# Two chained per-pixel channel mixes: four rows interleaved in SBUF, another way to layer 1's column matrices, fills at once, row products spread out

## The chip, the cores and the metric

The kernel runs on one core of a Trainium2 chip. A core has five engines that run on their own and wait for one another through semaphores: TensorE (PE; its weight loads are shown as PEld), VectorE (DVE), ScalarE (ACT), GpSimd (POOL) and SyncE (SP, which here issues all DMAs). The time is device microseconds of one execution. Kernel before: 859.1 us, median of 3 runs (857.77 to 862.08).

## The reference, cut to what matters

Two layers of the same form, each with its own factors, on x of 16 channels by 1024 rows (T) by 1024 columns (S), all float32:

```python
def layer(x, w, qw1, qw2, kw1, kw2, qdd, kdd):      # x: 1, 16, T, S ; M = N = 16, I = 2
    ret = einsum('BGMTS,GMN->BGNTS', x, w + eye)
    ret += einsum('BGITS,BTGIM->BGMTS', einsum('BGMTS,BTGIM->BGITS', x, qw1), qw2)   # per row t
    ret += einsum('BGITS,BSGIM->BGMTS', einsum('BGMTS,BSGIM->BGITS', x, kw1), kw2)   # per column s
    return ret + x * qdd[t] + x * kdd[s]
out = layer(layer(x, L0...), L1...)
```

So for each pixel (t, s) the 16 channels are multiplied by a 16x16 matrix that is a row matrix R[t] plus a column matrix C[s]. R[t] = qw1 qw2 (rank 2) plus the diagonal qdd; C[s] = kw1 kw2 (rank 2) plus w, the identity and the diagonal kdd.

## The kernel before, in words

**Tiling.** The rows are cut in 8 blocks of 128, a block in 16 chunks of 8 rows. The 1024 columns are cut in 8 eighths of 128 (`COLS`). A partition holds one channel of one eighth: 8 x 16 = 128 partitions. In the free dimension a chunk lies as [row group][column][row within the group], and `PAIR` rows make a group, here 2. One chunk is 4 KB a partition. `X` holds the block (and layer 0's result), `Y` the partial sums, `OUT` four slots for results.

**Four kinds of matmul.** A matmul's weights are small channel matrices placed on the diagonal of a larger one (`spread_quarter`, `spread_whole`: a compact row or column matrix times a mask).

- `t1(k, j)`: R of layer 0 on chunk j of block k. For each of 8 rows four matmuls of 64x64 weights on 64 columns, at the four quarters of the array. The moving columns of one row lie `PAIR` floats apart. Each matmul is two instructions, so 64 a chunk. ACT copies the result to `Y` (`t1_copies`).
- `s1(k, g)`: C of layer 0 on 4 of 64 column places, 16 matmuls of 64x64 weights on the block's 128 rows; the rows of one column lie in runs of `PAIR` floats. DVE adds the result to `Y` (`add_columns`).
- `s2(k, g)`: C of layer 1 on `Y`, the same shape; ACT copies it back to `X` (`s2_copies`).
- `t2(k, g)`: R of layer 1 on `Y`, whole 128x128 weights, 4 rows; DVE adds the result to what s2 left in `X` and writes `OUT` (`add_rows`).

A block's s phase is s1 and s2 in turn, 16 groups each, s2 two groups behind. Its t phase is, for each of 16 chunks, two t2 groups and the t1 chunk of the next block. The last t phase has no t1. PSUM banks are used in rings of two (PA for t1 and s2, PB for s1 and t2, where t2 takes four).

**Who makes the weights.** GpSimd makes WA (for t1, s2) and the odd WB, DVE the even WB, each four slots ahead.

**The queue of SP.** In the t phase, for each chunk: wait for DVE's row adds, store the chunk, load chunk o + 3 of the next block. After chunk 9 (`PROD_STORE`) it also waits for the next block's row products, stores both layers' products to DRAM and loads the next factors `QP`. At the s phase SP loads the first three chunks of the following block and reads the products back, replicated over the eighths, into `RT`. The products themselves (`products_of`: for each layer two multiplies, a sum, a diagonal add) stand in DVE's queue after chunk 6 (`PROD_STEP`).

**Start-up.** ACT writes w, the identity and kdd of all columns into `RS` (`base`). TensorE copies the factor kw2 from 8 partitions to 128 by a matmul with a selection matrix (`fill`, 512 values a time, 16 fills for two layers), DVE multiplies each by kw1 and adds it to RS (`column_unit`). Four fills come first, then one after each t1 chunk, since four banks of PB take them in turn.

Of the kernel before, what the change touches and what calls it, by code (L numbers as in the profile page):

```python
# [50 lines left out]
def cross_conv_kernel(nc, x, first_rows, row_params, col_left, col_right, w, products, out):  # L51
# [13 lines left out]
    with ctx:  # L65
# [374 lines left out]
        def _(dve):  # L440
# [31 lines left out]
            def row_matrices(l, before):  # L472
                shape = [P, CH, CH]
                q1, q2 = ([QP[:, l, (RANK * j + i) * CH:(RANK * j + i + 1) * CH] for i in range(RANK)]
                          for j in range(2))
                prod = PROD[:, l]
                for i in range(RANK):
                    nc.vector.tensor_tensor(prod[:, i], q1[i].unsqueeze(2).broadcast_to(shape),  # L478
                                            q2[i].unsqueeze(1).broadcast_to(shape), ALU.mult).then_inc(prod_step, 1)
                dve.wait_ge(prod_step, before + RANK)  # L480
                nc.vector.tensor_tensor(prod[:, 0], prod[:, 0], prod[:, 1], ALU.add).then_inc(prod_step, 1)  # L481
                dve.wait_ge(prod_step, before + RANK + 1)
                diagonal = prod[:, 0].rearrange("t c n -> t (c n)")[:, 0:CH * CH:CH + 1]
                nc.vector.tensor_tensor(diagonal, diagonal, QP[:, l, 2 * RANK * CH:PARAMS], ALU.add
                                        ).then_inc(prod_ready, 1)

            def products_of(number):
                dve.wait_ge(q_loaded, DMA * (number + 1))
                if not first(number):
                    dve.wait_ge(prod_stored, DMA * LAYERS * number)  # L490
                for l in range(LAYERS):
                    row_matrices(l, (RANK + 1) * (LAYERS * number + l))

# [240 lines left out]
```

## Time and profile before

| | before |
|---|---|
| median of 3 runs | 859.1 us |
| the profiled execution, and its span | 858.88 us, 857.1 us |
| PE busy / PEld busy | 766.5 / 704.4 us |
| DVE / POOL / ACT busy | 546.1 / 513.6 / 393.6 us |
| HBM read / written | 85.25 / 69.34 MB, 180 GB/s over the span |
| mean granted TensorE clock | 0.976 |

The span is the time from the first to the last instruction of the profiled execution; 1.8 us lie around it. Busy time of TensorE holds modelled ends of pipelined matmuls, so that the distance from one group's start to the next one's start is the better measure of its pace. The granted clock is 1.00 at 2.4 GHz and 0.50 at 1.2 GHz. A bracket at the end of a timeline row is the idle time ahead of it, and what ended it.

### The profile page before, as it was taken

What the parts mean: (1) busy time and instruction counts of PE and PEld (TensorE: products, weight loads), DVE (VectorE), ACT (ScalarE), POOL (GpSimd) and SP (SyncE); (2) the same over time, 40 slices, a digit from 0 to 9 for tenths busy, and PEclk for the clock granted to TensorE, in tenths of its full rate; (3) what the DMA queues carried; (4) which work ended last, traced back from release to release, by engine and by line L of the source; (5) the groups of instructions that cost most, each with busy time, mean ns of one, the idle gap of its engine ahead of it and who ended that gap; (6) DMA issues with size and microseconds to landing.
All of it is one profiled execution on the core that took longest, in us unless ns stands there. A gap on an engine that the chain in (4) does not pass through costs nothing.

```text
span 857.1 us, 42054 instructions
## 1 busy us (share of the span) xinstructions
PE 766.5 (89%) x18464; PEld 704.4 (82%) x18464; DVE 546.1 (64%) x809; ACT 393.6 (46%) x673; POOL 513.6 (60%) x456
## 2 busy tenths in 40 slices
PE   5998899799898999797998899979998889988998
PEld 2658799699787988797987898868998779877997
DVE  3338557468474866665676675837758566665668
ACT  6224563247432583225833466325743267324640
POOL 2326577467665677555766567646776567765733
PEclk9999999999999999989999999999999999999999
DMA  9804318952568618774098723785167840985026
GB/s 190 296 3 100 93 59 309 295 185 66 200 213 296 180 25 293 232 282 101 3 333 237 265 75 131 277 277 183 44 245 257 297 110 6 341 251 184 4 116 278
DMA packets 76045, 157.09 MB, mean 183 GB/s; under 512 B 39768, under 2 KB 40792, under 8 KB 73944
## 3 DMA queue, kind: packets, MB, share of 16 engines
q1 hardware_dynamic: 75888, 154.61, 55.5%
q8 instruction: 146, 2.39, 1.1%
q14 instruction: 11, 0.09, 0.0%
HBM read 85.25 MB, written 69.34 MB: 180 GB/s over the span
## 4 chain that ended last, share of the span: by engine, by line
POOL 34%; PE 25%; issue 24%; DVE 7%; DMA 5%; SPq 2%; POOLq 1%; ACT 1%; DVEq 0%; ACTq 0%
POOL WA L200 19%; POOL WB L208 9%; PE PB L655 7%; PE PA L607 7%; POOL WB L200 6%; PE PA L642 5%; PE PB L624 4%; DMA X<-in_x_dram 3%; DVE OUT L524 3%; PE PB L592 3%; DVE WB L208 2%; SPq L240 1%; DVE PROD L478 1%; DMA RT<-products 1%; DVE PROD L481 1%
## 5 line engine op out<-in xcount | busy, mean ns | idle before, releaser
L524 DVE TENSOR_TENSOR OUT<-PB,X 128x512 f32<-128x512 f32 x256 | 172.4, 686 | 185.0 <-PE PB L655 141.0
L402 ACT ACTIVATE Y<-PA 128x512 f32<-128x512 f32 (+1 forms) x256 | 147.3, 634 | 306.7 <-PE PA L607 306.7
L412 ACT ACTIVATE X<-PA 64x512 f32 (+3 forms) x384 | 232.7, 606 | 118.5 <-PE PA L642 111.8
L655 PE MATMUL PB<-Y,WB 128*128 128x128 f32 x2048 | 272.6, 286 | 1.7 <-issue 1.0
L655 PEld LDWEIGHTS PB<-Y,WB 128*128 128x128 f32 x2048 | 248.8, 193 | 15.8 <-issue 6.2
L208 POOL TENSOR_TENSOR WB<-RT,mask 128x512 f32<-128x512 f32 x128 | 156.3, 1221 | 106.1 <-PE PB L655 102.6
L511 DVE TENSOR_TENSOR Y<-PB,Y 128x512 f32 (+1 forms) x256 | 164.8, 685 | 80.7 <-PE PB L624 69.5
L607 PEld LDWEIGHTS PA<-X,WA 64*64 64x64 f32 x8192 | 149.4, 145 | 78.1 <-issue 37.8
L642 PE MATMUL PA<-Y,WA 64*64 64x128 f32 x4096 | 190.9, 311 | 20.7 <-issue 14.3
L607 PE MATMUL PA<-X,WA 64*64 64x64 f32 x8192 | 170.1, 234 | 44.0 <-DMA X<-in_x_dram 25.3
L200 POOL TENSOR_TENSOR WA<-RS,mask 128x512 f32<-128x512 f32 x128 | 139.4, 1089 | 110.7 <-PE PA L642 85.4
L624 PE MATMUL PB<-X,WB 64*64 64x128 f32 x4096 | 189.1, 311 | 14.6 <-DVE Y L511 9.3
L200 POOL TENSOR_TENSOR WA<-RT,mask 128x512 f32<-128x512 f32 x128 | 140.6, 1102 | 85.4 <-PE PA L607 47.1
L642 PEld LDWEIGHTS PA<-Y,WA 64*64 64x64 f32 x4096 | 163.7, 139 | 25.7 <-issue 16.4
L624 PEld LDWEIGHTS PB<-X,WB 64*64 64x64 f32 x4096 | 162.2, 139 | 18.7 <-issue 18.4
L208 DVE TENSOR_TENSOR WB<-RT,mask 128x512 f32<-128x512 f32 x128 | 102.8, 803 | 0.0
L200 POOL TENSOR_TENSOR WB<-RS,mask 128x512 f32<-128x512 f32 x64 | 80.7, 1262 | 33.6 <-PE PB L655 16.7
L200 DVE TENSOR_TENSOR WB<-RS,mask 128x512 f32<-128x512 f32 x64 | 69.2, 1082 | 0.0
L501 DVE TENSOR_TENSOR PB<-PB,RT 128x512 f32<-128x512 f32 x16 | 11.2, 700 | 31.1 <-PE PB L592 31.0
L478 DVE TENSOR_TENSOR PROD<-QP 128x256 f32<-128x256 f32 x32 | 22.3, 735 | 0.0
L592 PE MATMUL PB<-OUT,RT 8*128 8x512 f32 x16 | 15.4, 1104 | 5.4 <-DMA OUT<-in_right_dram 5.4
L419 ACT ACTIVATE RS<-RT,delta 128x128 f32<-128x128 f32 x32 | 12.5, 574 | 4.6 <-DVE RT L559 4.6
(24 smaller groups left out, 62.4 us busy)
## 6 DMA issues: line engine op xcount, KB each, us to landing
X<-in_x_dram SPq DMA_DIRECT2D x128, 512.0 KB, 6.0
out_dram<-OUT SPq DMA_DIRECT2D x128, 512.0 KB, 4.5
RT<-products SPq DMA_DIRECT2D x15, 1024.0 KB
products<-PROD SPq DMA_DIRECT2D x16, 128.0 KB, 8.2
RT<-products SPq DMA_DIRECT2D x1, 768.0 KB
QP<-in_rows_dram SPq DMA_DIRECT2D x8, 80.0 KB, 3.5
RT<-in_left_dram SPq DMA_DIRECT2D x1, 384.0 KB
RT<-products SPq DMA_DIRECT2D x1, 256.0 KB
```

Source lines behind the costliest of these rows:

```text
L200: engine.tensor_tensor(dst.rearrange("q (t a n) -> q t a n", t=CHUNK, a=PARTS), r, m, ALU.mult).then_inc(ready, 1)
L208: engine.tensor_tensor(dst.rearrange("q (t p n) -> q t p n", t=FEW, p=EIGHTHS), r, m, ALU.mult).then_inc(ready, 1)
L402: nc.scalar.activation(rows_of(Y, k, j)[:, :, WIDE * h:WIDE * (h + 1), :].rearrange("q a s c -> q a c s"), PA[HALVES * (j % RING) + h][:, ...
L412: nc.scalar.activation(columns_of(block_of(X, k), dst, WIDE * i + NARROW * g), by_columns(PA[HALVES * (g % RING) + i][src, :]), ACT.Copy). ...
L478: nc.vector.tensor_tensor(prod[:, i], q1[i].unsqueeze(2).broadcast_to(shape), q2[i].unsqueeze(1).broadcast_to(shape), ALU.mult).then_inc(p ...
L511: nc.vector.tensor_tensor(at, by_columns(PB[HALVES * (g % RING) + h][:, :]), at, ALU.add).then_inc(b_done, 1)
L524: nc.vector.tensor_tensor(rows(OUT[:, o % OUT_SLOTS]), PB[g % SLOTS][:, :].rearrange("q (a c s) -> q a c s", a=FEW2, c=PAIR), rows(rows_of ...
L592: nc.tensor.matmul(PB[u % FILLS][:, :], sel[0:EIGHTHS], KR[l][place // per][:, BANK * (place % per):BANK * (place % per + 1)], start=True, ...
L607: last = nc.tensor.matmul(PA[HALVES * (j % RING) + h][part(o), WIDE * r:WIDE * (r + 1)], matrix(WA[:, j % SLOTS], h, r), rows_of(X, k, j)[ ...
L624: last = nc.tensor.matmul(PB[HALVES * (g % RING) + h][part(o), ROWS * v:ROWS * (v + 1)] .rearrange("q (a c) -> q a c", c=PAIR), matrix(WB[ ...
L642: last = nc.tensor.matmul(PA[HALVES * (g % RING) + i][part(h ^ i), ROWS * v:ROWS * (v + 1)] .rearrange("q (a c) -> q a c", c=PAIR), matrix ...
L655: last = nc.tensor.matmul(PB[g % SLOTS][:, COLS * r:COLS * (r + 1)], WB[:, g % SLOTS, P * r:P * (r + 1)], rows_of(Y, k, t2_chunk(o))[:, (i ...
```

## The change: what it does

`PAIR` becomes 4: four rows are interleaved in X, Y and OUT, and in the host's layout of x and of the output. Counts of instructions in the two phases stay.

Layer 1's column matrices no longer go through TensorE. Its kw2 is loaded already replicated over the 16 channels (`load_right`, two DMAs of 1 MB) into the spare ends of Y and X, and DVE multiplies and adds there in operations of 1024 elements (`columns_of_layer1`). Layer 0's eight fills go into all eight banks at once, before the first t1.

The row products of the next block are one operation per chunk, from chunk 2 to chunk 9 (`product_op`), and are stored after chunk 11.

```diff
-PAIR = 2
+PAIR = 4
-UNITS = LAYERS * QUARTERS * RANK
-FILLS = 4
+UNITS = QUARTERS * RANK
+SIDE = COLS // 2
-PROD_STEP = 6
-PROD_STORE = 9
+PROD_FIRST = 2
+PROD_OPS = 4
+PROD_STORE = 11
...
+            def load_right(h):
+                sp.dma_start(KR1[h].rearrange("q i s n -> q (i s n)"),
+                             col_right1[h].unsqueeze(1).broadcast_to([EIGHTHS, CH, RANK * SIDE * CH])
+                             ).then_inc(right_loaded[1 + h], DMA)
...
-            for h in range(2):
-                load_right(1, h, right_loaded[1 + h])
-            load_q(0)
             load_x(0, 1)
             sp.wait_ge(first_stored, DMA)
             load_rows(BLOCKS * LAYERS, 0, 0, FIRST_ROWS, rt_first)
             load_x(0, 2)
             load_rows(BLOCKS * LAYERS, 0, FIRST_ROWS, ROWS - FIRST_ROWS, rt_loaded[0])
-            for j in range(3, CHUNKS):
+            load_x(0, 3)
+            for h in range(len(KR1)):
+                load_right(h)
+            load_q(0)
+            for j in range(4, CHUNKS):
                 load_x(0, j)
...
+            def columns_of_layer1(h):
+                shape = [P, SIDE, CH]
+                part = slice(SIDE * h, SIDE * (h + 1))
+                dve.wait_ge(right_loaded[1 + h], DMA)
                 for i in range(RANK):
+                    chained(nc.vector.tensor_tensor(KR1[h][:, i], KL[:, 1, i, part].unsqueeze(2).broadcast_to(shape),
+                                                    KR1[h][:, i], ALU.mult))
+                chained(nc.vector.tensor_tensor(KR1[h][:, 0], KR1[h][:, 0], KR1[h][:, 1], ALU.add))
+                dve.wait_ge(base_ready, LAYERS * CH)
+                nc.vector.tensor_tensor(RS[:, 1, part, :], KR1[h][:, 0], RS[:, 1, part, :], ALU.add
+                                        ).then_inc(rs1_done, 1)
...
-                    if more and o == PROD_STEP:
-                        products_of(k + 1)
+                    n = o - PROD_FIRST
+                    if more and 0 <= n < LAYERS * PROD_OPS:
+                        product_op(k + 1, n // PROD_OPS, n % PROD_OPS)
...
+            for u in range(RING * HALVES):
+                unit_product(u)
             for u in range(UNITS):
-                column_unit(u)
+                unit_sum(u)
+                if RING * HALVES + u < UNITS:
+                    unit_product(RING * HALVES + u)
+            dve.wait_ge(right_done, UNITS)
             for g in range(0, SLOTS, 2):
                 s1_weights(nc.vector, g, wb_even)
-            products_of(0)
+            for n in range(LAYERS * PROD_OPS):
+                product_op(0, n // PROD_OPS, n % PROD_OPS)
+            for h in range(len(KR1)):
+                columns_of_layer1(h)
...
             pe.wait_ge(sel_ready, 1)
-            for u in range(FILLS):
+            pe.wait_ge(right_loaded[0], DMA)
+            for u in range(UNITS):
                 fill(u)
             for j in range(CHUNKS):
                 t1(0, j)
-                if FILLS + j < UNITS:
-                    fill(FILLS + j)
```

TensorE at the start, before. L592 is a fill (its bank PB, its source in OUT), L607 a matmul of t1.

```order
L592 MATMUL PB<-OUT,RT 128x512 [waits right_loaded0,sel_ready]
L592 MATMUL PB<-OUT,RT 128x512 [waits right_loaded0] x3
L607 MATMUL PA<-X,WA 64x64 [waits wa_ready,x_loaded0]
L607 MATMUL PA<-X,WA 64x64 x31
L592 MATMUL PB<-OUT,RT 128x512 [waits right_done,right_loaded0]
L607 MATMUL PA<-X,WA 64x64 [waits wa_ready,x_loaded1]
L607 MATMUL PA<-X,WA 64x64 x31
L592 MATMUL PB<-OUT,RT 128x512 [waits right_done,right_loaded0]
L607 MATMUL PA<-X,WA 64x64 [waits a_done,wa_ready,x_loaded2]
```

The same place after the change; the fill is L625 now, t1 is L642.

```order
L625 MATMUL PA<-OUT,RT 128x512 [waits right_loaded0,sel_ready]
L625 MATMUL PA<-OUT,RT 128x512 x3
L625 MATMUL PB<-OUT,RT 128x512 x4
L642 MATMUL PA<-X,WA 64x64 [waits right_done,wa_ready,x_loaded0]
L642 MATMUL PA<-X,WA 64x64 x31
L642 MATMUL PA<-X,WA 64x64 [waits right_done,wa_ready,x_loaded1]
L642 MATMUL PA<-X,WA 64x64 x31
L642 MATMUL PA<-X,WA 64x64 [waits a_done,wa_ready,x_loaded2]
```

No fill stands between two t1 chunks any more; the first two chunks wait for DVE's sums (`right_done`), whose banks they take.

SP at start-up, before: `Y<-in_right_dram` and `X<-in_right_dram` are layer 1's factors, 8 partitions each, and `QP` the row factors.

```order
L240 DMA products<-RT 128x16x16 [waits first_prod]
L233 DMA Y<-in_right_dram 8x2048
L233 DMA X<-in_right_dram 8x2048
L236 DMA QP<-in_rows_dram 128x160
L223 DMA X<-in_x_dram 128x1024
L243 DMA RT<-products 128x1x512 [waits first_stored]
L223 DMA X<-in_x_dram 128x1024
L243 DMA RT<-products 128x1x1536
L223 DMA X<-in_x_dram 128x1024 x13
```

And after; the factors now go to 128 partitions.

```order
L245 DMA products<-RT 128x16x16 [waits first_prod]
L226 DMA X<-in_x_dram 128x1024
L248 DMA RT<-products 128x1x512 [waits first_stored]
L226 DMA X<-in_x_dram 128x1024
L248 DMA RT<-products 128x1x1536
L226 DMA X<-in_x_dram 128x1024
L236 DMA Y<-in_right_dram 128x1x2048
L236 DMA X<-in_right_dram 128x1x2048
L241 DMA QP<-in_rows_dram 128x160
L226 DMA X<-in_x_dram 128x1024 x12
```

Both factor loads and the row factors moved behind x 1 to 3 and RT, and they stand ahead of x 4 to 15.

DVE in a t phase, before, around the row products (L478 multiply, L481 sum, L484 diagonal; L524 is a row add, L208 makes weights).

```order
L524 TENSOR_TENSOR OUT<-PB,X 128x2x2x128 [waits b_full]
L478 TENSOR_TENSOR PROD<-QP 128x256 [waits prod_stored,q_loaded]
L478 TENSOR_TENSOR PROD<-QP 128x256
L481 TENSOR_TENSOR PROD<-PROD 128x256 [waits prod_step]
L484 TENSOR_TENSOR PROD<-PROD,QP 128x16 [waits prod_step]
L478 TENSOR_TENSOR PROD<-QP 128x256 x2
L481 TENSOR_TENSOR PROD<-PROD 128x256 [waits prod_step]
L484 TENSOR_TENSOR PROD<-PROD,QP 128x16 [waits prod_step]
L524 TENSOR_TENSOR OUT<-PB,X 128x2x2x128 [waits stored3,b_full]
```

After the change, three of the eight (L495 sum, L499 diagonal, L491 multiply; L553 is a row add, L211 makes weights).

```order
L553 TENSOR_TENSOR OUT<-PB,X 128x4x128 [waits b_full]
L495 TENSOR_TENSOR PROD<-PROD 128x256 [waits prod_step]
L553 TENSOR_TENSOR OUT<-PB,X 128x4x128 [waits stored1,b_full]
L211 TENSOR_TENSOR WB<-RT,mask 128x512
L553 TENSOR_TENSOR OUT<-PB,X 128x4x128 [waits b_full]
L499 TENSOR_TENSOR PROD<-PROD,QP 128x16 [waits prod_step]
L553 TENSOR_TENSOR OUT<-PB,X 128x4x128 [waits stored2,b_full]
L211 TENSOR_TENSOR WB<-RT,mask 128x512
L553 TENSOR_TENSOR OUT<-PB,X 128x4x128 [waits b_full]
L491 TENSOR_TENSOR PROD<-QP 128x256
```

Between two product operations stand two row adds and one set of weights.

## Rows read from the trace of the kernel before

**Rows 1.** The page: busy time of each engine, share of the span.
```profile
PE 766.5 (89%) x18464; PEld 704.4 (82%) x18464; DVE 546.1 (64%) x809; ACT 393.6 (46%) x673; POOL 513.6 (60%) x456
```

**Rows 2.** Windows: stretch, length, busy time by engine, PEclk, DMA share, GB/s.
```profile
28.00:36.00 8.00, 8.00 (x133) 4.58 (x132) 2.78 (x4) 2.26 (x4) 3.55 (x4) 1.00 1.03 409
40.00:64.00 24.00, 24.00 (x404) 13.94 (x406) 8.35 (x13) 6.77 (x12) 6.24 (x6) 1.00 0.06 22
84.00:102.00 18.00, 13.72 (x343) 13.15 (x338) 9.40 (x15) 9.17 (x16) 9.03 (x8) 0.91 0.47 129
119.44:178.91 59.47, 52.91 (x1285) 49.38 (x1285) 35.56 (x56) 19.50 (x34) 35.59 (x32) 0.94 0.75 256
178.91:218.40 39.49, 37.77 (x1037) 36.90 (x1029) 30.56 (x41) 28.07 (x47) 27.61 (x25) 1.00 0.40 110
821.70:857.10 35.40, 31.20 (x260) 29.65 (x256) 29.58 (x46) 2.37 (x4) 14.84 (x14) 1.00 0.59 238
```

**Rows 3.** Timeline of start-up, GpSimd and TensorE: start, length, engine, line, operation.
```profile
26.44 3.03 POOL L200 TENSOR_TENSOR WA<-RT,mask 128x512 f32<-128x512 f32 x3 [6.73 <-DMA RT<-products]
...
50.08 2.07 PE L592 MATMUL PB<-X,RT 8*128 8x512 f32 x2
52.08 1.99 PE L607 MATMUL PA<-X,WA 64*64 64x64 f32 x64
53.99 2.07 PE L592 MATMUL PB<-X,RT 8*128 8x512 f32 x2
...
76.35 1.99 PE L624 MATMUL PB<-X,WB 64*64 64x128 f32 x32 [3.85 <-DVE Y L511]
78.09 1.77 PE L642 MATMUL PA<-Y,WA 64*64 64x128 f32 x32
```

**Rows 4.** Timeline of TensorE, first s phase (L624, L642) and t phase.
```profile
82.01 1.35 PE L624 MATMUL PB<-X,WB 64*64 64x128 f32 x32
83.17 1.34 PE L642 MATMUL PA<-Y,WA 64*64 64x128 f32 x32
...
119.44 2.08 PE L655 MATMUL PB<-Y,WB 128*128 128x128 f32 x16
121.45 1.17 PE L607 MATMUL PA<-X,WA 64*64 64x64 f32 x64
122.55 2.08 PE L655 MATMUL PB<-Y,WB 128*128 128x128 f32 x16
```

**Rows 5.** Timeline of TensorE, the waits of the first t phase.
```profile
154.56 1.17 PE L607 MATMUL PA<-X,WA 64*64 64x64 f32 x64 [1.37 <-DMA X<-in_x_dram]
...
169.13 1.99 PE L607 MATMUL PA<-X,WA 64*64 64x64 f32 x64 [4.93 <-DMA X<-in_x_dram]
171.05 3.78 PE L655 MATMUL PB<-Y,WB 128*128 128x128 f32 x16
174.76 1.22 PE L607 MATMUL PA<-X,WA 64*64 64x64 f32 x64
```

**Rows 6.** Groups by form: count, busy us and mean ns, idle before.
```profile
L402 ACT ACTIVATE Y<-PA 128x512 f32<-128x512 f32 x220 | 126.7, 634 | 277.4 <-PE PA L607 277.4
L419 ACT ACTIVATE RS<-RT,delta 128x128 f32<-128x128 f32 x32 | 12.5, 574 | 4.6 <-DVE RT L559 4.6
L452 DVE TENSOR_REDUCE delta<-ident 128x16 f32<-128x128 f32 x1 | 0.4, 354 | 0.0
L451 DVE TENSOR_REDUCE mask<-ident 128x8 f32<-128x128 f32 x1 | 0.3, 286 | 1.7 <-POOL ident L371 1.7
```

**Rows 7.** Timeline of DVE and of SP's queue, around the first products.
```profile
141.14 1.02 DVE L478 TENSOR_TENSOR PROD<-QP 128x256 f32<-128x256 f32 x2
...
146.27 0.68 DVE L524 TENSOR_TENSOR OUT<-PB,X 128x512 f32<-128x512 f32 x1
...
148.17 0.34 SPq L227 DMA_DIRECT2D out_dram<-OUT  x1
...
153.43 6.32 SPq L240 DMA_DIRECT2D products<-PROD  x2
```

More of the change, by code:

```diff
@@ L48, with cross_conv_kernel @@
 S1_ADDS = 2
-def cross_conv_kernel(nc, x, first_rows, row_params, col_left, col_right, w, products, out):
+def cross_conv_kernel(nc, x, first_rows, row_params, col_left, col_right0, col_right1, w, products, out):
     f32 = mybir.dt.float32
@@ L384, in _ @@
             pool.wait_ge(right_done, UNITS)
+            pool.wait_ge(rs1_done, len(KR1))
             for g in range(SLOTS):
@@ L470, in first_matrices, with product_op @@
                                         ).then_inc(first_prod, 1)
-            def row_matrices(l, before):
+            def product_op(number, l, n):
                 shape = [P, CH, CH]
-                q1, q2 = ([QP[:, l, (RANK * j + i) * CH:(RANK * j + i + 1) * CH] for i in range(RANK)]
-                          for j in range(2))
                 prod = PROD[:, l]
-                for i in range(RANK):
[L478 to L492, printed above, removed]
[L494 to L505 removed]
+                before = (RANK + 1) * (LAYERS * number + l)
@@ new lines, in product_op @@
+                if l == 0 and n == 0:
+                    dve.wait_ge(q_loaded, DMA * (number + 1))
+                    if not first(number):
+                        dve.wait_ge(prod_stored, DMA * LAYERS * number)
+                if n < RANK:
+                    q1, q2 = (QP[:, l, (RANK * j + n) * CH:(RANK * j + n + 1) * CH] for j in range(2))
+                    nc.vector.tensor_tensor(prod[:, n], q1.unsqueeze(2).broadcast_to(shape),
+                                            q2.unsqueeze(1).broadcast_to(shape), ALU.mult).then_inc(prod_step, 1)
+                elif n == RANK:
+                    dve.wait_ge(prod_step, before + RANK)
+                    nc.vector.tensor_tensor(prod[:, 0], prod[:, 0], prod[:, 1], ALU.add).then_inc(prod_step, 1)
+                else:
+                    dve.wait_ge(prod_step, before + RANK + 1)
+                    diagonal = prod[:, 0].rearrange("t c n -> t (c n)")[:, 0:CH * CH:CH + 1]
+                    nc.vector.tensor_tensor(diagonal, diagonal, QP[:, l, 2 * RANK * CH:PARAMS], ALU.add
+                                            ).then_inc(prod_ready, 1)
```

64 lines of the change are left out of this document (33 added, 31 removed).

## The prediction

> **What bounds the kernel now.** I read the page first, then the stages, then TensorE's own rows. TensorE is busy for 766.5 of 857.1 us, VectorE (DVE) for 546.1, GpSimd for 513.6 and ScalarE (ACT) for 393.6 [rows 1], so only TensorE can set the whole. The stages [rows 2] have different limits.
>
> - Start-up, to about 78 us. TensorE alternates a fill (2.00 us, 50.08 to 52.08) and a t1 chunk (1.91, to 53.99), 3.91 us in all [rows 3]. The granted clock stands as 1.00 there, but t1 spans 1.99 us as it does in the slow stretch at 169 us, against 1.17 elsewhere [rows 3 to 5]. I take the engine to be at its lower level, 1.2 GHz, and the column as blank before its first record. From 40 to 64 us the DMA queues stand idle (share 0.06 [rows 2]): twelve fills between the chunks, not a transfer, make this stage long. Then DVE works through eight row products before its first column add, for which TensorE waits 3.85 us [rows 3].
> - Eight s phases (the second: 39.49 us [rows 2]): s1 and s2 groups 1.165 us apart [rows 4]. 32 of them are 37.3 us; 2.2 are waits at the two ends.
> - Seven t phases with t1 (the first: 59.47 us [rows 2]). A chunk is t2 2.01 plus t1 1.10 = 3.11 us [rows 4], 16 are 49.8, so about 10 us are stall: x late by 1.37 and by 4.93 us, behind the latter the lower clock (t2 3.71 us for 2.01 [rows 5]), and smaller ones. Both transfers and TensorE are near full: 256 GB/s over the phase [rows 2].
> - The last t phase, 35.40 us, has no t1, and DVE is busy 29.58 of it [rows 2].
>
> **Four rows interleaved.** Counts and sizes of matmuls, copies and transfers stay. What changes is how far apart an engine's successive elements lie. In s1, s2 and their copies a run of two floats becomes a run of four. In t1, t2, their copies and the row adds the step grows from 8 to 16 bytes.
>
> *The s side.* A group is 8 quads of four 64x64 tiles: 1.165/8 = 146 ns a quad at 2.4 GHz. At the lower clock the next group starts after 1.74 us (76.35 to 78.09 [rows 3]), 217 ns a quad, and 128 columns x 2 cycles are 213. At 2.4 GHz the arithmetic needs 107, so 39 ns belong to a limit that does not follow the clock: 0.61 ns for each of the 64 runs. t1 shows less of it: 16 quads in 1.10 us, 69 ns with the change of stage, where 53 are arithmetic. Half as many runs should halve the 39: 126 ns, 1.01 us a group. Ends: nothing, or down to the next engine, which is DVE with 30.56 us busy in the phase [rows 2]; with 2.2 us of ends that is 32.8 for 39.49, or 54 us in eight phases. I take 0.156 us x 28 groups x 8 = **-35 us**, leaving out two groups at each end, which wait for others.
>
> *The t side on TensorE.* No row has a moving read with one float per 16 bytes. The nearest is t2 at 8 bytes: 16 instructions in 2.01 us at the high clock and in 3.71 at the low one, 126 and 232 ns each, both 19 ns over their arithmetic (107 and 213). So at 8 bytes nothing limits the reading. One column per 0.83 ns is what it needs; an s run of two takes up to 146/64 = 2.28 ns. Ends: 0, and 2.28 ns a column, which makes t2 292 ns and a t1 quad 146, +3.9 us a chunk, some 450 us in all. I take 0, by the 8-byte row, and keep the rest as rivals.
>
> The Trainium skill (Advanced Engine Details and Errata, Memory Cachelines) says that SBUF has 16-byte lines and that it takes two hits on a line for full speed; the t reads would fall from two hits to one, and by it the t side loses more than the s side wins. The skill's SBUF page (SBUF — State Buffer, Door 1: The DMA port swizzle) also words the free step as up to 4 fp32, by which 16 bytes would cost nothing. The trace has only the case of two hits, so it does not decide between them.
>
> *The t side on DVE and ACT.* DVE's reduction of 128 elements takes 354 ns at a 64-byte step and 286 contiguous [rows 6]: 0.53 ns an element more, so at most 272 ns on each row add of 0.68 us (146.27 [rows 7]). In a t phase that is 32 x 0.27 = 8.7 us on DVE's 35.56 [rows 2], 44 of 50 us, covered; in the last phase DVE is nearly the limit and 8.7 would show. I take half, **+4 us**. Bounds 0 and +60: ACT needs 574 ns for 128 elements at a 64-byte step, 634 for 512 at 8 bytes [rows 6]. Its two copies are 1.27 of 3.11 us, so 1.5 us a copy would still be hidden, and 1.7 would not (rival 4).
>
> **Start-up.** Eight fills at once take 13.7 us (each 2 x 512 columns x 2 cycles at 1.2 GHz), four took half of it, and the other twelve at 2.00 us go from between the chunks. Chunks 0 to 3 are done by 27, and GpSimd gets the rest of RT at 26.44 [rows 3]. Then comes the new load: SP issues 2 x 1 MB of replicated factors ahead of q and of x 4 to 15. They have the shape of RT's loads (eight replicas outermost), and two of those are what moves from 84 to 102 us, 129 GB/s at a share of 0.47 [rows 2]: 8.4 us each, on half of the engines. So the factors land at about 36 and 44 us, x 4 behind them at 45.5, and x 15 at 60 (twelve x 1.28 us, 524 KB at the rate of x alone, 409 GB/s [rows 2]). t1 keeps pace. s1 begins at 61.5, now 70.0. DVE gets q at 45, needs 7.5 us for the products (as now) and then eight operations of 1024 elements. 512 take 0.68 us (146.27) and 256 some 0.5 (two in 1.02 at 141.14 [rows 7]), about 0.5 more for each 512: 1.2 us, 9.6 in all, to 62. GpSimd waits for these and makes its first six matrices in 7.6 us. The first s2 group starts at 67, not at 78.09: **-11 us**, with the 3.85 us wait in it. Ends: -3 if the factors hold the queues for 25 us, -18 if they run beside x.
>
> **Products one per chunk, stored two chunks later.** Now the eight operations hold DVE from 141.14 to 146.27, and SP, which waits for the adds behind them, issues its next store at 148.17 [rows 7]; x 10 is late by 1.37 us [rows 5]. That goes. The store's own cost does not: SP spends 6.32 us on issuing it [rows 7], and x 13, next in its queue, costs 4.93. After the change x 13 and 14 are ahead of the store and x 15 behind it, three chunks before its use, as x 13 was. The stall moves; only the backlog is shorter. I take 2 us a phase (1.4 of the row above, the rest from the backlog), 7 x 2 = **-14 us**; ends 0 and -25.
>
> **Sum.** The profiled execution took 858.88 us (span 857.1 and 1.8 around it), 0.2 under the median of the runs, 859.1. 858.88 - 35 + 4 - 11 - 14 = 802.9: **803 us**.
>
> **Rivals.**
> 1. *One float per line halves the moving read* of t1 and t2 (the slower side). Place: every t chunk. Twice the column time makes t2 232 ns and a t1 quad 122: 128 chunks x 1.71 + 112 x 0.85 = +314 us. Off go 35, 11 and 70 us of stalls (7 x 10) that slower chunks cover: 1057. From 116/128 = 0.9 us more per chunk on it turns the gain into a loss. For it: s reads show a limit at two floats per line. Against: t2 at two floats shows none. It is what the skill's rule of two hits would do.
> 2. *Only t1 is slowed*, since its tiles read two streams from each partition: 64 lines in 53 to 69 ns now, 0.95 ns each, so 128 take 122 ns, +0.85 us x 112 = 95. Less 35, 11 and 60 it is 848, within 830 to 885.
> 3. *The s limit is not in the runs*, and four are read no faster than two: 803 + 35 = 838.
> 4. *ACT's copies set the t pace* at 1.7 us each (3 ns an element, as the 64-byte row allows after 190 ns of fixed time): 3.4 us a chunk and 0.4 for the hand-over, 61 us a phase for 57.5, and the 11 of start-up are gone: 803 + 25 + 11, about 840.
>
> **How the numbers follow.** Forecast 0.48 (780 to 825), rival 1 0.15, rival 2 0.15, rival 3 0.12, rival 4 0.10. About 0.5% (4 us) is what a measurement can tell from no change. Faster are the forecast, rival 3 and about a third of the rest outside rival 1 (0.09): 0.69; same 0.05; slower 0.26. The range 775 to 890 leaves out rival 1 and thin tails.
>
> **What would show it.** s groups 1.01 us apart (1.165 refutes the first term); t2 and t1 spans of 2.08 and 1.17 us (3.7 and 2.0 with the clock at 1.00 are rival 1); row adds between 0.68 and 0.96 us, ACT's t copies under 1.5; the first s2 near 67 us with t1 held for x 4 till about 45; the longest wait of a t phase at its last t1, none after a burst of products. The forecast falls if a t chunk grows by 0.9 us, or if the factors hold x beyond 70 us.

## The result: 28% slower, every t chunk nearly doubled

Before: 860.59 us, the median of four runs on the chip of the comparison (857.77 to 863.77). After: 1099.93 us (1098.39 to 1103.63). The ratio is 1.279, with the interval 1.273 to 1.285. I had predicted 803 us, within 775 to 890. What came is close to rival 1, to which I had given 0.15 and 1057 us. Medians and ranges in this document take in every run, while the ratios leave out five that lie in the chip's slower state (one each of e3, e10 and e11, two of e9, the profiled one among them).

The page of the kernel after: busy time, the chain by engine, and the costliest groups (busy us, mean ns of one, idle before). It answers to [rows 1, 6].

```profile
PE 1010.7 (92%) x18448; PEld 893.4 (81%) x18448; DVE 614.2 (56%) x801; ACT 497.3 (45%) x673; POOL 489.8 (45%) x456
...
PE 78%; issue 8%; POOL 6%; DMA 4%; ACT 2%; DVE 1%; SPq 0%; POOLq 0%; DVEq 0%; ACTq 0%
...
L690 PE MATMUL PB<-Y,WB 128*128 128x128 f32 x2048 | 492.6, 409 | 0.0
L553 DVE TENSOR_TENSOR OUT<-PB,X 128x512 f32<-128x512 f32 x256 | 276.0, 1078 | 358.5 <-PE PB L690 314.0
L410 ACT ACTIVATE Y<-PA 128x512 f32<-128x512 f32 (+1 forms) x256 | 255.5, 1109 | 456.2 <-PE PA L642 456.2
```

TensorE is busy for 244 us more, and DVE and ACT together for 172 us more. Their counts of row adds and copies are the same, but each takes longer: 1.08 us for a row add of 0.68, 1.11 for a t copy of 0.63 [rows 6, 7]. The chain of waits is TensorE's for 78%. The t copies and adds lie beside it: their engines idle for 358 and 456 us ahead of them.

TensorE's timeline after, in the first t phase (L690 is t2, L642 t1); it answers to [rows 4]:

```profile
117.69 3.87 PE L690 MATMUL PB<-Y,WB 128*128 128x128 f32 x16
121.49 2.06 PE L642 MATMUL PA<-X,WA 64*64 64x64 f32 x64
123.48 3.87 PE L690 MATMUL PB<-Y,WB 128*128 128x128 f32 x16
```

From start to start, t2 takes 3.80 us for 2.01 and t1 1.99 for 1.10: a chunk is 5.79 us for 3.11. These are the sizes that I had named for rival 1 (3.7 and 2.0).

Windows of the kernel after: the whole first t phase, and most of the second s phase (length, busy time by engine, PEclk, DMA share, GB/s); compare [rows 2]:

```profile
117.69:210.37 92.68, 92.68 (x1284) 80.33 (x1284) 46.31 (x56) 32.37 (x35) 33.79 (x32) 1.00 0.50 164
210.37:248.00 37.63, 32.28 (x1005) 30.87 (x1000) 27.39 (x40) 27.24 (x45) 25.83 (x24) 0.91 0.36 116
```

In the t phase TensorE never stops: the waits for x [rows 5] are gone, since transfers have time (a share of 0.50 for 0.75), and the granted clock is 1.00 throughout. Its 92.68 us are 16 chunks of 5.79. Adding up the two traces by phase, from the first instruction of each phase to that of the next:

| stretch | before, us | after, us | difference |
|---|---|---|---|
| start to the first s phase | 70.0 | 81.1 | +11.1 |
| eight s phases | 344.4 | 305.9 | -38.5 |
| seven t phases with t1 | 407.4 | 648.8 | +241.4 |
| last t phase | 35.3 | 62.5 | +27.2 |
| span | 857.1 | 1098.4 | +241.3 |

The cut between the first two stretches hides something. The first s phase took 49.4 us before, with the slow stretch at 84 to 102 us in it [rows 2], and takes 36.5 now. So 12.9 of the 38.5 us are won there, and the first t phase starts at 117.7 us for 119.4: start-up and first s phase together are 1.8 us shorter.

### The profile page after: what moved, and what is told of

It is laid out like the page before. It is cut to its first block, busy times and chain, and to the rows that moved or that the text cites. A ratio compares the mean times of both kernels' runs of the same rounds, so it can differ in the third digit from the quotient of the medians.

```text
span 1098.4 us, 41981 instructions
## 1 busy us (share of the span) xinstructions
PE 1010.7 (92%) x18448; PEld 893.4 (81%) x18448; DVE 614.2 (56%) x801; ACT 497.3 (45%) x673; POOL 489.8 (45%) x456
## 4 chain that ended last, share of the span: by engine, by line
PE 78%; issue 8%; POOL 6%; DMA 4%; ACT 2%; DVE 1%; SPq 0%; POOLq 0%; DVEq 0%; ACTq 0%
PE PB L690 43%; PE PA L642 21%; PE PA L677 7%; PE PB L659 6%; POOL WA L203 4%; DMA X<-in_x_dram 3%; POOL WB L203 2%; ACT Y L410 2%; ACT X L420 1%; POOL WB L211 0%; DVE Y L540 0%; DMA products<-RT 0%; DMA RT<-in_first_dram 0%; SPq L248 0%; SPq L236 0%
## 5 line engine op out<-in xcount | busy, mean ns | idle before, releaser
L690 PE MATMUL PB<-Y,WB 128*128 128x128 f32 x2048 | 492.6, 409 | 0.0
L553 DVE TENSOR_TENSOR OUT<-PB,X 128x512 f32<-128x512 f32 x256 | 276.0, 1078 | 358.5 <-PE PB L690 314.0
L410 ACT ACTIVATE Y<-PA 128x512 f32<-128x512 f32 (+1 forms) x256 | 255.5, 1109 | 456.2 <-PE PA L642 456.2
L690 PEld LDWEIGHTS PB<-Y,WB 128*128 128x128 f32 x2048 | 412.2, 206 | 53.4 <-issue 20.6
L642 PEld LDWEIGHTS PA<-X,WA 64*64 64x64 f32 x8192 | 232.9, 152 | 72.6 <-issue 48.4
L642 PE MATMUL PA<-X,WA 64*64 64x64 f32 x8192 | 264.0, 292 | 29.4 <-DMA X<-in_x_dram 23.7
L211 POOL TENSOR_TENSOR WB<-RT,mask 128x512 f32<-128x512 f32 x128 | 143.2, 1119 | 309.8 <-PE PB L690 307.2
L659 PE MATMUL PB<-X,WB 64*64 64x128 f32 x4096 | 160.0, 282 | 27.9 <-DVE Y L540 16.6
L677 PE MATMUL PA<-Y,WA 64*64 64x128 f32 x4096 | 162.2, 282 | 21.0 <-issue 14.7
L659 PEld LDWEIGHTS PB<-X,WB 64*64 64x64 f32 x4096 | 138.5, 140 | 33.1 <-issue 32.9
L677 PEld LDWEIGHTS PA<-Y,WA 64*64 64x64 f32 x4096 | 138.7, 140 | 28.8 <-issue 21.1
L211 DVE TENSOR_TENSOR WB<-RT,mask 128x512 f32<-128x512 f32 x128 | 95.5, 746 | 0.0
L491 DVE TENSOR_TENSOR PROD<-QP 128x256 f32<-128x256 f32 x32 | 13.2, 418 | 26.0 <-DMA QP<-in_rows_dram 26.0
L625 PE MATMUL PA<-OUT,RT 8*128 8x512 f32 x8 | 7.2, 1072 | 5.1 <-DMA OUT<-in_right_dram 5.1
L625 PEld LDWEIGHTS PA<-OUT,RT 8*128 8x128 f32 x8 | 2.5, 325 | 8.2 <-issue 8.2
```

The costliest lines, as they stand in the source:

```text
L211: engine.tensor_tensor(dst.rearrange("q (t p n) -> q t p n", t=FEW, p=EIGHTHS), r, m, ALU.mult).then_inc(ready, 1)
L410: nc.scalar.activation(rows_of(Y, k, j)[:, :, WIDE * h:WIDE * (h + 1), :].rearrange("q a s c -> q a c s"), PA[HALVES * (j % RING) + h][:, ...
L491: nc.vector.tensor_tensor(prod[:, n], q1.unsqueeze(2).broadcast_to(shape), q2.unsqueeze(1).broadcast_to(shape), ALU.mult).then_inc(prod_st ...
L553: nc.vector.tensor_tensor(rows(OUT[:, o % OUT_SLOTS]), PB[g % SLOTS][:, :].rearrange("q (a c s) -> q a c s", a=FEW2, c=PAIR), rows(rows_of ...
L642: last = nc.tensor.matmul(PA[HALVES * (j % RING) + h][part(o), WIDE * r:WIDE * (r + 1)], matrix(WA[:, j % SLOTS], h, r), rows_of(X, k, j)[ ...
L659: last = nc.tensor.matmul(PB[HALVES * (g % RING) + h][part(o), ROWS * v:ROWS * (v + 1)] .rearrange("q (a c) -> q a c", c=PAIR), matrix(WB[ ...
```

## Experiments

The first four settle which edit and which engine; the next four measure reading patterns by themselves; the last three try what the measurements suggest. "ns per quad" or "per instruction" is the median from the start of one to the start of the next, in the trace. Where a ratio stands, it is to the kernel before in runs on the same chip (865.78 us for e1 to e3, 865.41 for e9 to e11).

### e1: everything but the interleave of four

```diff
-PAIR = 4
+PAIR = 2
```

> The changed kernel with two rows interleaved again; start-up, products and all else as changed. Theory 1 (TensorE's reads at one float per 16-byte line cost twice the time): the t phases return to 55 to 60 us (from 92.7) and the last one to 35, the s groups to 1.165 us; 268 us come off, 38 go back on: about 865 us. Theory 2 (the other parts of the change, start-up or products, caused a good part of the 239 us): it stays above 900 us. The start-up alone should show s1 beginning at 70 us or later, since x 4 waits behind the factors here too.

Measured: 835.62 us (830.49 to 836.46), ratio 0.962 (0.957 to 0.968). TensorE's timeline, a t chunk and the longest wait of the first t phase with t1:

```profile
117.99 2.08 PE L690 MATMUL PB<-Y,WB 128*128 128x128 f32 x16
120.01 1.17 PE L642 MATMUL PA<-X,WA 64*64 64x64 f32 x64
121.10 2.08 PE L690 MATMUL PB<-Y,WB 128*128 128x128 f32 x16
...
172.68 1.99 PE L642 MATMUL PA<-X,WA 64*64 64x64 f32 x64 [3.36 <-DMA X<-in_x_dram]
```

The chunk is 3.11 us again, and theory 1 stands, though the time is 30 us under the 865 that I expected. The other three edits are worth 3.8%. Seven t phases fall from 407.4 to 387.0 us, 2.9 each, where I had put 2 for the products' placing. The longest wait for x in the first of them went from 4.93 us, in mid-phase [rows 5], to 3.36, at the last t1; over the seven, TensorE's waits for x fall from 25.3 to 15.1 us. The eight s phases take 332.1 us for 344.4 without any interleave of four, and 10.1 of these 12.3 us lie in the first one (39.3 for 49.4). The first t phase starts at 118.0 us, for 119.4 before, so start-up and the first s phase gained 1.4 us, not 11.

### e2: the interleave of four alone, in the kernel before

```diff
-PAIR = 2
+PAIR = 4
```

> The kernel before with nothing but PAIR = 4. Theory 1: t phases of 92 to 95 us, s groups of 0.87 us; 860 + 268 - 38 = about 1090 us. Theory 2: clearly under 1050 us, with the rest owed to start-up and products.

Measured: 1095.85 us (1091.98 to 1098.78), ratio 1.265 (1.259 to 1.271). TensorE's timeline, one t2:

```profile
113.09 3.88 PE L655 MATMUL PB<-Y,WB 128*128 128x128 f32 x16
116.89 2.06 PE L607 MATMUL PA<-X,WA 64*64 64x64 f32 x64
```

This one number is the whole loss. Every t phase takes 92.7 us here as in the kernel after, the last 62.5. The other three edits, worth 3.8% in e1, cost another 1.4% beside the interleave: with them the ratio is 1.279, without them 1.265. The long t phases have no stall left for them to shorten, and the first t phase starts at 107.3 us here for 117.7 with them.

### e3: only TensorE's t reads put back to 8 bytes

The layout stays interleaved by four, for DVE and ACT too. t1 and t2 read as many floats, at a step of 8 bytes.

```diff
+def near(chunk, r, first, count):
+    at = 2 * COLS * (r // 2) + 2 * first + r % 2
+    return chunk.rearrange("q a s c -> q (a s c)")[:, at:at + 2 * count - 1:2]
...
-rows_of(X, k, j)[part(h), r // PAIR, WIDE * o:WIDE * (o + 1), r % PAIR],
+near(rows_of(X, k, j)[part(h)], r, WIDE * o, WIDE),
-rows_of(Y, k, t2_chunk(o))[:, (inner + r) // PAIR, :, (inner + r) % PAIR],
+near(rows_of(Y, k, t2_chunk(o)), inner + r, 0, COLS),
```

> The changed kernel, but t1 and t2 read their moving columns 8 bytes apart (wrong columns of the same chunk; the output is not the reference's). ACT and DVE still work at 16 bytes. Theory 1: t2 and t1 go back to 2.0 and 1.1 us a chunk; DVE with 2 x 1.08 + 0.68 = 2.84 us (3.3 with a product) is then near the limit: t phases of 50 to 57 us, the last one 46, about 830 us in all. Theory 3 (ACT's and DVE's slower copies hold the t phase, TensorE's rows only show the waiting): t phases stay near 92 us.

Measured: 827.04 us (823.35 to 839.18), ratio 0.951 (0.946 to 0.956). So some 270 us (1098.4 to 826.4 between the spans of the profiled executions) hang on the step of TensorE's moving operand alone. Row adds stay at 1082 ns and t copies at 1123. What these cost shows beside e1, where both are fast: the seven t phases are 405.5 us for 387.0, with 40.1 us of waits for x for 15.1, and the last phase is 45.5 us for 35.3. SP asks for the next x behind a wait for DVE's row adds, which fits, but no run separates DVE from ACT in it. The last phase, TensorE's timeline and DVE's:

```profile
787.84 2.23 PE L695 MATMUL PB<-Y,WB 128*128 128x128 f32 x16 [0.33 <-DVE WB L211]
790.39 2.22 PE L695 MATMUL PB<-Y,WB 128*128 128x128 f32 x16 [0.32 <-DVE WB L211]
```
```profile
808.15 2.05 DVE L553 TENSOR_TENSOR OUT<-PB,X 128x512 f32<-128x512 f32 x2
810.13 0.67 DVE L211 TENSOR_TENSOR WB<-RT,mask 128x512 f32<-128x512 f32 x1
810.73 2.01 DVE L553 TENSOR_TENSOR OUT<-PB,X 128x512 f32<-128x512 f32 x2
```

TensorE starts a chunk each 2.55 us and waits before each for a matrix of DVE's. DVE has no gap: two adds and one matrix from 808.15 to 810.73 are 2.58 us.

### e4: no interleave at all, in the kernel before

`PAIR = 1`: an s run is one float, 512 bytes from the next. Theory "lines" counts 16-byte lines; theory "distance" says that the s side already pays for how far apart they lie.

> The kernel before with PAIR = 1: t reads contiguous, s reads single floats 512 bytes apart, the mirror of the change. Theory 1, by lines alone: a quad of s goes from 146 to 213 ns or a little more, a group to 1.75 us, + 0.58 x 256 = 150 us, about 1010. If distance between lines costs more as well (2.28 ns a run as with runs of two): quads of 292 ns, + 300 us. t1 and t2 stay at 1.10 and 2.0 us a chunk.

Measured once: 1128.8 us. TensorE's s groups, and the groups of the s phase's DVE and ACT:

```profile
103.79 2.56 PE L642 MATMUL PA<-Y,WA 64*64 64x128 f32 x32
106.09 2.56 PE L624 MATMUL PB<-X,WB 64*64 64x128 f32 x32
```
```profile
L412 ACT ACTIVATE X<-PA 64x512 f32 (+3 forms) x384 | 398.5, 1038 | 230.6 <-PE PA L642 224.0
...
L511 DVE TENSOR_TENSOR Y<-PB,Y 128x512 f32 (+1 forms) x256 | 314.4, 1281 | 172.3 <-PE PB L624 172.3
```

A group is 2.30 us, 289 ns a quad (four 64x64 tiles side by side): twice the 146 of two floats a run, and not the 213 of lines alone. The t side, contiguous now, does not gain: t2 112 ns and t1 59, as at 8 bytes.

### e5: sixteen reading patterns, one stream

In the last t phase of the kernel before, t2's 16 groups each read in another pattern. `far` is the step in floats, `run` how many lie together.

```diff
+flat = block_of(buf, k)[lines].rearrange("q a s c -> q (a s c)")
+if run == 1: return flat[:, 0:far * (count - 1) + 1:far]
+return flat[:, 0:far * count].rearrange("q (n f) -> q n f", f=far)[:, :, 0:step * (run - 1) + 1:step]
```

> The kernel before; in the last t phase t2 reads its 128 moving floats in sixteen patterns, two groups of four matmuls each (wrong columns, so the output is not the reference's). Patterns in order: single floats 4, 8, 12, 16, 32, 64 and 512 bytes apart; pairs 16, 64 and 1024 bytes apart; fours 32 and 2048 bytes apart; pairs whose two floats are 8 bytes apart, each pair 16 bytes on; pairs 24, 32 and 256 bytes apart. Theory 1 (a line of 16 bytes costs 1.67 ns, a float 0.83): 107 to 114 ns an instruction wherever a line gives two or more, 213 to 227 for single floats 16 bytes or more apart, about 160 to 170 at 12 bytes (96 lines). Rival (it is the step that counts: full speed up to 8 bytes, half from more): 12 bytes costs as much as 16. A second rival (distance costs too): pairs 1024 bytes apart are slower than pairs 16 bytes apart.

Windows, each from the first of eight instructions to the first of the next eight (an instruction that began earlier is counted too): 8, 12 and 16 bytes, then pairs 1 KB apart.

```profile
823.61:824.52 0.91, 0.91 (x10) 1.00 0.00 0
827.05:828.43 1.38, 1.38 (x9) 1.00 0.89 356
828.43:830.24 1.81, 1.81 (x10) 1.00 0.73 285
...
846.41:847.31 0.90, 0.90 (x11) 1.00 0.73 296
```

| one 128-column instruction reads | ns |
|---|---|
| single floats at 4, 8 bytes | 112, 114 |
| at 12 bytes | 173 |
| at 16, 32, 64, 512 bytes | 227, 233, 218, 220 |
| pairs each 16, 24, 32, 64, 256, 1024 bytes | 114, 113, 116, 112, 112, 112 |
| fours each 32, 2048 bytes | 112, 112 |

(The sixteenth pattern reads the same floats as 8 bytes does, written as pairs: 114.) Counting the 16-byte lines that a pattern touches sorts all of them. At 16 bytes there are 128 lines in 227 ns, 1.77 ns a line; at 8 bytes 64 lines in 114, 1.78; at 12 bytes 96 lines in 173, 1.80. Fewer lines than 64 don't help: 32 lines take 112, near the 107 of the arithmetic. The rival of the step alone falls with 12 bytes (173, not 227), that of distance with the pairs. Distance is all but free for one stream (218 to 233 ns from 16 to 512 bytes), which no theory of mine had said in this form.

### e6: the same patterns as 64x64 quads, two streams

As e5, with each instruction replaced by a quad as in the s phases: each of the four tiles reads 64 partitions, so that every partition is read by two tiles at once. These are the two streams.

> The same sixteen patterns in the last t phase, but read by quads of 64x64 tiles as s1 does, two streams from each partition (another computation, the output is not the reference's). If two streams share one limit, patterns that a single stream reads at full speed are slower here: pairs 1024 bytes apart near 146 ns a quad as in the s phase. If 146 ns come from distance alone, pairs 16 bytes apart take 107 to 116 and pairs 64, 256 and 1024 apart more. Single floats 16 bytes apart: 213 to 233 by theory 1.

Windows, eight quads each: single floats 16 and 512 bytes apart, pairs 1 KB apart, fours 2 KB apart.

```profile
838.50:840.33 1.83, 1.83 (x37) 1.00 0.71 287
847.56:849.82 2.26, 2.26 (x39) 1.00 0.18 63
...
855.85:857.02 1.17, 1.17 (x42) 1.00 0.77 305
859.38:860.25 0.87, 0.87 (x40) 1.00 0.20 57
```

At small steps two streams cost what one does (109, 114, 173, 229 ns for 4, 8, 12, 16 bytes). Far apart they don't: pairs 1 KB apart take 146 ns for 112 and single floats at 512 bytes 289 for 220. Pairs at 64 bytes take 115, at 256 bytes 146. Fours 2 KB apart take 109. This is the s limit, and the 289 ns are e4's: not the run alone, but two streams in short runs that lie far apart. A quad differs from e5's instruction in the size of its tiles as well, and that was not tested apart from the number of streams.

### e7: steps of the row adds and of ACT's copies

In the kernel after, by chunk: DVE's output and addend strided (16 bytes) or contiguous, ACT's output at 16 bytes, contiguous, at 64 and at 8 bytes.

```diff
+written, read = ((rows, rows), (rows, flat), (flat, rows), (flat, flat))[o % 4]
```

> The changed kernel; the row adds of chunk o take, by o mod 4, both operands in SBUF at 16 bytes, the read contiguous, the write contiguous, both contiguous; ACT's t copies write, by chunk mod 4, at 16 bytes, contiguous, at 64 and at 8 bytes (wrong places within the chunk). If DVE's extra 392 ns and ACT's 475 are the cost of one line per element: DVE 1078 with both strided, 686 with both contiguous, and the read or the write alone shows which one pays; ACT 1109 at 16 and 64 bytes alike, 634 at 8. If distance counts, ACT's 64 bytes costs more than its 16.

Timelines of ACT (two copies each, at 16 bytes, contiguous, at 64 bytes) and of DVE (addend contiguous, output contiguous, both):

```profile
252.16 2.00 ACT L422 ACTIVATE Y<-PA 128x512 f32 x2 [3.51 <-PE PA L656]
257.93 1.09 ACT L422 ACTIVATE Y<-PA 128x512 f32 x2 [3.77 <-PE PA L656]
263.73 1.92 ACT L422 ACTIVATE Y<-PA 128x512 f32 x2 [4.71 <-PE PA L656]
```
```profile
253.97 1.07 DVE L567 TENSOR_TENSOR OUT<-PB,X 128x512 f32<-128x512 f32 x1 [2.45 <-PE PB L704]
...
259.77 1.06 DVE L567 TENSOR_TENSOR OUT<-PB,X 128x512 f32<-128x512 f32 x1 [2.90 <-PE PB L704]
...
265.57 0.69 DVE L567 TENSOR_TENSOR OUT<-PB,X 128x512 f32<-128x512 f32 x1 [2.58 <-PE PB L704]
```

Medians: ACT 1107, 595, 1058 and 634 ns; DVE 1076 with both strided, 1077 and 1065 with one, 692 with none. One strided operand costs DVE all that two do.

### e8: how far is far, for pairs in two streams

As e6 with runs of two throughout, the distance varied. Theory A: only multiples of 256 bytes are slow. Theory B: everything from 256 bytes on is.

> The kernel before; in the last t phase sixteen distances between the pairs that the quads read, two groups each (another computation, the output is not the reference's). Bytes from pair to pair, in order: 128, 192, 256, 384, 512, 768, 264, 272, 288, 320, 1024, 1032, 1040, 1056, 1088, 1152. Theory A (two streams of one partition meet where successive lines lie a multiple of 256 bytes apart): 144 to 147 ns a quad at 256, 512, 768 and 1024, 109 to 116 at all others. Theory B (any distance from 256 bytes up costs): 144 to 147 from 256 on, whatever the remainder.

Windows, eight quads each, for pairs 256, 272, 1024 and 1040 bytes apart:

```profile
834.75:835.89 1.14, 1.14 (x40) 1.00 0.58 223
...
845.71:846.62 0.91, 0.91 (x41) 1.00 0.97 383
851.68:852.85 1.17, 1.17 (x34) 1.00 1.01 413
...
855.94:856.87 0.93, 0.93 (x41) 1.00 1.02 414
```

256, 512, 768 and 1024 bytes take 146 ns; 192, 272, 288, 320, 1040, 1056 and 1088 take 110 to 116. (For 128 and 192 bytes only seven and eight quads count; for the others of theirs the granted clock was 0.50, and each took 213.) Theory B falls. Theory A holds at its four distances, but something smaller stands beside it, which it had excluded: 264 and 1032 bytes take 120 to 122, and the odd multiples of 128 (128, 384, 1152) 123 to 130.

### e9: e1 with the factors laid out for all DMA engines

The replicated factors stand in DRAM as 128 rows, and are loaded without the broadcast.

```diff
-col_right1[h].unsqueeze(1).broadcast_to([EIGHTHS, CH, RANK * SIDE * CH])
+col_right1[h]
...
+right1 = _np.repeat(right1.reshape(2, EIGHTHS, RANK * SIDE * CH), CH, axis=1)
```

> e1, and layer 1's factors lie in DRAM already repeated for the 16 channels, so that the two loads go to 128 partitions from 128 rows. If it was the eight-row form that made them last 23 us (half of the engines), they take 5 to 7 us in all, x 4 lands near 33 us, s1 begins at 50 to 60 us for 78.6, and the time is some 20 us under e1: 815. If the 2 MB themselves cost it, nothing changes.

Measured: 827.33 us (816.82 to 838.72), ratio 0.946 (0.941 to 0.950). Its timeline of DVE, where the q that lies behind the factors in SP's queue has arrived:

```profile
34.47 0.76 DVE L491 TENSOR_TENSOR PROD<-QP 128x256 f32<-128x256 f32 x2 [9.74 <-DMA QP<-in_rows_dram]
```

In e1 that stands at 49.63 us after a wait of 25.13. The two loads land 5 us after the x ahead of them, as expected. The first s phase starts at 65.2 us for 78.6 (61.2 and 62.3 in e10 and e11, which have the same loads), but not at the 50 to 60 that I expected, and the ratio to the kernel before is 0.017 lower than e1's: 14 us, not 20.

### e10 and e11: e9 with padded lines

Pairs 1 KB apart become pairs 1040 bytes apart (e10) or 1032 (e11).

```diff
+LINE = COLS + 2
-X = sb("X", [P, ALL, COLS, PAIR])
+X = sb("X", [P, ALL, LINE, PAIR])
```

Y likewise, x in DRAM with it, and the products' buffer smaller to make room. e11 has `COLS + 1`.

> e9 with two columns of padding after each row pair's 128 in X and Y, so that the pairs of a column lie 1040 bytes apart and not 1024 (the padding travels with x, 1.6% more bytes; the products' scratch and the identity share room to make place). Theory A: quads of 109 to 116 ns, s groups of 0.90 us for 1.165, the phase 32 to 35 us for 40: 8 x 6 = some 45 us under e9, about 770. Theory B: no change from e9.

> As e10, with one column of padding: 1032 bytes. Theory A, if any remainder will do: as e10. If a whole line of 16 bytes of remainder is needed, between e9 and e10. Theory B: as e9.

Measured: e10 803.81 us (796.37 to 809.42), ratio 0.931 (0.926 to 0.936); e11 806.61 (803.09 to 819.42), ratio 0.928 (0.924 to 0.933). The two can't be told apart by time. By the ratios e10 is 13 us under e9, where I expected 45. In the traces e10's s quad takes 115 ns and e11's 122, as e8 had them, and the s phases 301.0 and 314.3 us. Page and TensorE's timeline of e10:

```profile
PE 694.4 (87%) x18448; PEld 640.2 (81%) x18448; DVE 536.2 (67%) x801; ACT 405.0 (51%) x673; POOL 516.7 (65%) x456
...
PE 44%; issue 15%; DMA 10%; ACT 10%; POOL 8%; DVE 7%; SPq 5%; ACTq 1%; DVEq 0%; POOLq 0%
```
```profile
66.39 1.14 PE L660 MATMUL PB<-X,WB 64*64 64x128 f32 x32
67.32 1.13 PE L678 MATMUL PA<-Y,WA 64*64 64x128 f32 x32
68.23 1.31 PE L660 MATMUL PB<-X,WB 64*64 64x128 f32 x29
```

An s group is 0.92 us for 1.165 [rows 4], and the t side keeps its 8 bytes (114 and 59 ns). So theory A's mechanism holds and its price doesn't. Beside e1, e10's s phases are 31 us shorter (301.0 for 332.1), though TensorE idles in them for 37.9 us and not 21.9, and its seven t phases are 10 us longer (396.9 for 387.0). e10 and e11 are the fastest versions here, 7% under the kernel before: the s side's gain without the t side's loss. TensorE is busy for 694.4 us now, and the chain of waits is TensorE's for less than half.

## Why the prediction was wrong

**The step that failed** is the t side on TensorE: "I take 0, by the 8-byte row." It was +2.68 us a chunk. In seven phases that is 112 x 2.68 = 300 us, less the 59 us of stalls that the kernel before had (407.4 - 7 x 49.8) and that longer chunks cover: +241, as measured; the last phase adds 27. The row was read rightly and stretched too far. t2 at 8 bytes took its arithmetic and a little over at both clocks, and I wrote that nothing limits the reading there. But where one cost is just covered by another, the row can't show it: at 8 bytes 64 lines cost 114 ns and the arithmetic 107. Twice the lines had to be paid in full (e5: 227 ns). The other end of my range, +3.9 us, came from the s row, and that was too high since the s side's quads pay for lines that lie a multiple of 256 bytes apart as well (e6, e8). The case between the ends, the doubling, was on the table as rival 1. The rule that I weighed there (the Trainium skill, Advanced Engine Details and Errata, Memory Cachelines: 16-byte lines, two hits on each for full speed) is what e5 shows, 227 ns with one hit and 114 with two. The other wording that I weighed (the Trainium skill, SBUF — State Buffer, Door 1: The DMA port swizzle: a step of up to 4 fp32 is free) does not hold for this read, which takes 173 ns at 3 fp32 already. I gave the doubling 0.15 when a rule and an end of the range both pointed at it.

**Rival 1's own sum** was 43 us short of the 1100. By the table's stretches, the chunk grew by 2.68 and not 2.56 (13 us), start-up lost 11 instead of winning 11 (22), the stalls to be covered were 59 and not 70 (11), and the s side gave 3.5 more. That is 43. Rival 2 fell with t2, rival 3 with the s groups, rival 4 with the chain, where ACT's copies of 1.11 us stay under the 1.5 at which I had them hidden.

**The s side, -35: -26 by the interleave**, near by luck of two errors. The -38.5 of the table holds the 12.3 us that e1 has without the interleave; between e1 and the kernel after the s phases fall from 332.1 to 305.9 us, and between the kernel before and e2 from 344.4 to 314.2. A group is 0.874 us, not 1.01, so 28 groups alone would give 8 x 28 x 0.291 = 65 us. The mechanism was not half the cost for half the runs, but all of it: fours cost nothing even in two streams (e6). Some 39 us of this were given back. TensorE's timeline after, at the second s phase (L659 s1, L677 s2):

```profile
214.46 1.34 PE L659 MATMUL PB<-X,WB 64*64 64x128 f32 x32 [2.16 <-DVE Y L540]
215.50 2.00 PE L677 MATMUL PA<-Y,WA 64*64 64x128 f32 x32
217.21 1.77 PE L659 MATMUL PB<-X,WB 64*64 64x128 f32 x32
218.77 1.08 PE L677 MATMUL PA<-Y,WA 64*64 64x128 f32 x32
219.64 1.08 PE L659 MATMUL PB<-X,WB 64*64 64x128 f32 x32
```

DVE comes late from its slower row adds, TensorE waits 2.16 us, and behind the wait come two groups at the pace of the lower clock (1.71 and 1.56 us from start to start) before the 0.87 of the higher one. The waits from 210.37 to 248.00 are 5.4 us in all. Windows over all eight s phases have TensorE idle for 22 us in e1 (309.91 busy of 332.12) and for 49 in the kernel after (256.95 of 305.90), and the granted clock at 0.50 for 17 and 34 us. So 27 of the 39 us are waits, and by the quads' paces (213 ns at the lower clock for 109 or 146) the lower clock costs 11 more. I had put the ends at nothing or at DVE; of the waits, those for DVE's sums in Y grew by 14 us (3.0 to 16.6), and about as much is put down to nothing that the profile shows.

**DVE and ACT, +4 within 0 to +60.** A row add grew by 0.39 us where I allowed 0.27 at most, a t copy by 0.48. TensorE's longer chunks cover both in the kernel after. e3 takes that cover away, and beside e1 they cost 29 us: 10 in the last phase, where the prediction had placed them, and 19 in the seven t phases, where it had called them covered.

**Start-up, -11: +8 to the same mark**, the first s2 group (78.09 us before, forecast 67, now 86.50); +11 to the first s1. Timelines of the kernel after, of DVE, TensorE and SP's queue:

```profile
50.23 0.76 DVE L491 TENSOR_TENSOR PROD<-QP 128x256 f32<-128x256 f32 x2 [26.02 <-DMA QP<-in_rows_dram]
```
```profile
51.27 3.98 PE L642 MATMUL PA<-X,WA 64*64 64x64 f32 x128 [21.56 <-DMA X<-in_x_dram]
...
86.50 0.47 PE L677 MATMUL PA<-Y,WA 64*64 64x128 f32 x3
```
```profile
13.00 38.34 SPq L226 DMA_DIRECT2D X<-in_x_dram  x12
53.05 12.60 SPq L245 DMA_DIRECT2D products<-PROD  x2
```

The factors arrive at about 49 us, five later than I had them, and x 4 at 51.3 for 45.5. SP has asked for all of x 4 to 15 by 51.34, and they land 1.3 us apart, the last at 66.0 for 60. So the queue is six us late.

The larger part is the step "t1 keeps pace": the twelve chunks from x 4 on take 29.9 us (51.27 to 81.14), 2.5 each, where x comes every 1.3. A t1 of 1.99 us stood in my own rows [rows 3]. The versions whose t1 reads at 8 bytes need about as long: 27.9 us in e1, 28.8 to 29.4 in e9, e10 and e11, although in these three x 4 lands 15 to 18 us earlier. Two things are seen there: a lower granted clock (0.83 in the mean in the kernel after, 0.72 in e1), and gaps: in the kernel after 1.8 us of waits for ACT's copies of 1.1 us and 3.6 that the profile puts down to nothing, in e1 8.0 of the latter. What these are stays open. DVE's eight column operations (1.2 to 2.0 us each, predicted 1.2) end at 66 and delay nothing, since the last Y arrives at 83. That start-up and first s phase together are still no longer than before is owed to the latter, as e1 shows. e9 confirms the factors' part: spread over all DMA engines they bring q 15 us and the s phase 13.4 us forward.

**Products, -14: about -20** over seven phases in e1. As predicted, the wait for x did not go but moved to the last t1 and got shorter (4.93 to 3.36 us). Half of the 20 are such waits (25.3 to 15.1 us); the granted clock, at 0.50 for 13.5 us of these phases and not 27.2, gives some 7 more. That it is the placing and not another of e1's edits was not tested apart. In the kernel after there is no wait for x in these phases, so the term is nothing there.

## What to carry to other kernels

Before changing how rows are interleaved, count for every fp32 moving read how many of its floats share a 16-byte line: two is the least at which it was free here, and a row at exactly two shows no sign that it is at the edge. A change that lengthens one reader's run lengthens the other's step. Padding the line by 16 bytes gave the first most of what it wanted and left the second's pace as it was. Where a rule predicts a step just beyond the last point that the trace shows, that last point is no evidence against it.

## What the runs showed of the hardware

- A moving fp32 read costs TensorE 1.77 to 1.80 ns per 16-byte line touched, or its arithmetic, whichever is longer (e5); for one stream the lines' distance hardly matters (218 to 233 ns for 128 lines 16 to 512 bytes apart). At 1.2 GHz a t1 quad with one float a line takes 116 ns, as at 2.4 GHz, though its arithmetic goes from 53 to 107: that limit does not follow the clock.
- Quads of 64x64 tiles, two of which read each partition, cost 1.3 times as much when successive lines are a multiple of 256 bytes apart (146 for 112 ns in pairs, 289 for 220 in single floats), nothing at 272 or 1040 bytes, and 1.05 to 1.15 at 264, 1032 and odd multiples of 128 bytes (e6, e8). Fours 2 KB apart take 109 all the same: at the 146/64 = 2.28 ns a line of such pairs, their 32 lines would stay under the arithmetic (an estimate).
- A step of 16 bytes in either SBUF operand makes DVE's add of 512 elements 1.07 us for 0.69; ACT's copy takes 0.60 us contiguous, 0.63 at 8 bytes, 1.11 at 16 and 1.06 at 64 (e7). For DVE that is 0.75 ns an element, where the reduction at a 64-byte step had let me expect 0.53 at most.
- Issuing the same two stores of products took SP 12.60 us in start-up behind the factors and twelve chunks of x (DMA share 0.61 over it), 6.32 in the first t phase before (1.01) [rows 7], 4.10 at 188.11 us of the kernel after (0.93), and 1.35 at 75.05 us of the kernel before, whose queues had stood idle (0.01 from 64 to 75 us). What sets it was not tested.
